# Wider query and key pieces in two attention stages, and the first stage's row normalisation on POOL

## What is computed

```
x = x + 0.5 * ffn0(layernorm(x))     stage 0, "f0": 512 -> 1536 -> 512, silu(gate) * up, weights rounded through fp8
x = x + attn0(layernorm(x))          stage 1, "a0": 16 query heads, 4 key/value heads of 32, a rotary factor, biases
x = x + 0.5 * ffn0(layernorm(x))     stage 2, "f0", same weights
x = x + 0.5 * ffn1(layernorm(x))     stage 3, "f1": 512 -> 2048 -> 512
x = x + attn1(layernorm(x))          stage 4, "a1": 16 query and 16 key/value heads
x = x + 0.5 * ffn1(layernorm(x))     stage 5, "f1"
layernorm(x) = (x - mean) / sqrt(var + 1e-5);   attention is causal, softmax over keys
```

## Time and profile before

| | |
|---|---|
| median of 3 runs | 2639.78 us (2636.49 to 2643.28) |
| the profiled execution's own time | 2630.22 us |
| its span, first to last instruction | 2628.5 us |
| mean granted TensorE clock | 0.994 |
| busy: PE, DVE, ACT, POOL | 2530.7, 1528.6, 1045.8, 966.4 us |
| stage 0 begins its products | 33.3 us |
| a0: opening from 299.6, last of it about 795 us | |
| a1: opening from about 1570, last of it about 2100 us | |

### The profile page before, as it was taken

How to read it: one execution, slowest core, us unless ns; L and a number is a source line. 1 busy time by engine, 2 the same in 40 slices (tenths; PEclk the granted TensorE clock), 3 DMA queues, 4 the chain that set the end, 5 groups by cost and what they waited for, 6 DMA issues and landing times.

```text
span 2628.5 us, 44135 instructions
## 1 busy us (share of the span) xinstructions
PE 2530.7 (96%) x16928; PEld 2010.6 (76%) x16928; DVE 1528.6 (58%) x3356; ACT 1045.8 (40%) x1901; POOL 966.4 (37%) x1357
## 2 busy tenths in 40 slices
PE   6999989989999999999999999999999899999999
PEld 4788867667668888888888878777777678888887
DVE  7777579979975445433333345798589643333333
ACT  7555346655653223311111133566466431111111
POOL 3333566766644225211111122666366521111110
PEclk9999999999999999999999999999999999999999
DMA  4222031132220110100000002342133100000001
GB/s 148 73 73 73 31 83 46 51 72 61 50 90 1 37 45 14 36 25 25 24 25 25 24 17 58 92 97 73 48 93 78 38 33 25 24 25 25 25 16 64
DMA packets 72002, 128.73 MB, mean 49 GB/s; under 512 B 15728, under 2 KB 24944, under 8 KB 71792
## 3 DMA queue, kind: packets, MB, share of 16 engines
q1 hardware_dynamic: 71792, 125.92, 16.9%
HBM read 62.42 MB, written 13.63 MB: 29 GB/s over the span
## 4 chain that ended last, share of the span: by engine, by line
PE 80%; DVE 8%; ACT 2%; POOL 2%; SPq 2%; DMA 2%; issue 2%; DVEq 0%; ACTq 0%; POOLq 0%
PE psum L1045 65%; PE psum L1163 4%; PE psum L1126 4%; PE psum L1144 4%; DVE psum L1495 2%; PE psum L1174 2%; SPq L1726 1%; PE psum L1054 1%; DVE s1a0rden L1534 1%; SPq L1745 1%; DVE s4a1rden L1534 1%; ACT s1a0e L1329 0%; DVE stats L1361 0%; POOL rstd L1604 0%; PE psum L1133 0%
## 5 line engine op out<-in xcount | busy, mean ns | idle before, releaser
L1495 DVE CUSTOM_DVE_ANT_0 psum<-psum,mask_q 128x512 f32<-128x512 f32 (+5 forms) x768 | 413.3, 575 | 100.0 <-PE psum L1126 97.0
L1045 PE MATMUL psum<-hA_hi,wmem 128*128 128x256 f32 (+1 forms) x1536 | 405.5, 334 | 0.5 <-DVE s1a0negmax L1495 0.3
L1045 PEld LDWEIGHTS psum<-hA_hi,wmem 128*128 128x128 f32 x1536 | 270.3, 191 | 32.0 <-DVE s1a0negmax L1495 1.5
L1045 PE MATMUL psum<-hA_lo,wmem 128*128 128x512 f32 (+1 forms) x864 | 293.8, 340 | 0.0
L1329 ACT ACTIVATE s4a1e<-psum,p_scale 128x384 f32<-128x384 f32 (+5 forms) x384 | 205.1, 579 | 92.2 <-PE psum L1144 88.8
L1448 DVE SCALAR_TENSOR_TENSOR x<-psum,x 128x512 f32<-128x512 f32 x256 | 175.8, 689 | 97.2 <-PE psum L1045 93.8
L1329 ACT ACTIVATE s1a0e<-psum,p_scale 128x384 f32<-128x384 f32 (+5 forms) x384 | 201.9, 577 | 76.3 <-PE psum L1144 74.9
L1419 DVE TENSOR_TENSOR s5f1prod<-psum,s5f1silu 128x512 f32<-128x512 f32 x64 | 44.3, 692 | 302.1 <-PE psum L1045 302.1
L1419 DVE TENSOR_TENSOR s3f1prod<-psum,s3f1silu 128x512 f32<-128x512 f32 x64 | 44.3, 692 | 294.1 <-PE psum L1045 294.1
L1616 POOL TENSOR_TENSOR wmem<-raw,wmem 128x512 fp32r<-128x512 f32 x58 | 74.2, 1289 | 314.8 <-ACT wmem L1231 314.7
L1045 PE MATMUL psum<-s3f1w,s3f1a 128*128 128x512 f32 x768 | 181.5, 390 | 0.9 <-POOL s3f1w L1616 0.9
(11 more groups left out here) (194 smaller groups left out, 5568.3 us busy)
## 6 DMA issues: line engine op xcount, KB each, us to landing
s1a0qst<-s1a0qs SPq DMA_DIRECT2D x96, 128.0 KB, 2.4
s4a1qst<-s4a1qs SPq DMA_DIRECT2D x96, 128.0 KB, 2.4
s4a1kst<-s4a1ks SPq DMA_DIRECT2D x96, 128.0 KB, 2.4
raw<-in_gate SPq DMA_DIRECT2D x44, 256.0 KB, 2.9
raw<-in_up SPq DMA_DIRECT2D x44, 256.0 KB, 2.8
raw<-in_down SPq DMA_DIRECT2D x44, 256.0 KB, 2.8
rounded<-s0f0w SPq DMA_DIRECT2D x24, 256.0 KB, 2.0
s2f0w<-rounded SPq DMA_DIRECT2D x24, 256.0 KB, 4.8
```

The costliest lines, as they stand in the source:

```text
L1045: ins = pe.matmul(out_, w, m, start=n == 0, stop=n == len(terms) - 1)
L1495: dve.tensor_tensor_reduce(scores, scores, mask_q[:, first:first + pw], -1.0, -MASKED, ALU.add, ALU.min, T[s]["negmax"][n % 2][:, column:c ...
```

## The change

Pieces become 512 columns wide: two for each name and group where there were four. Products, `turned`, `piece_out` and `piece_lo` each work on 512 columns, with unchanged arithmetic. In the units a piece starts every 4 units where it was every 2; the norm jobs of groups 2 and 6 start one unit earlier. In the opening the guard now holds back the second of two q pieces. Waits that named piece 1 or 3 name the one that covers the same columns. In stage 0 alone `ln_norm` is done by POOL (one `tensor_scalar` of 128x512, multiply then add) and no longer by ACT. The bank model's durations follow.

```diff
+PIECE = 512
+QK_PIECES = SEQ // PIECE
-NORMS_FROM = 11
+NORMS_FROM = 10
-PIECE_STEP = 2
+PIECE_STEP = 4
...
             return [timed((0, ("piece", s, g, n, i)),
...
-                    for i in range(4) for n in names_of_group(s, g)]
+                    for i in range(QK_PIECES) for n in names_of_group(s, g)]
...
-            if norms.busy(last_norm[s, 1]) and any(("piece", s, 0, "q", 2) in job[0]
+            if norms.busy(last_norm[s, 1]) and any(("piece", s, 0, "q", QK_PIECES // 2) in job[0]
...
-            done["norm", s, where[0]] = work("act", 0.81, ("stats", s, where[0]))
+            done["norm", s, where[0]] = work("pool" if s == 0 else "act", 1.3 if s == 0 else 0.81,
+                                             ("stats", s, where[0]))
...
-            done[step] = work("pe", 1.4, *banks)
+            done[step] = work("pe", 1.4 * PIECE / 256, *banks)
...
+        def normed_by_pool(s):
+            return s == 0
...
             def piece(s, g, n, i):
-                cols = slice(i * CH // 2, (i + 1) * CH // 2)
+                cols = slice(i * PIECE, (i + 1) * PIECE)
...
-                products(ps[:, 0, 0:CH // 2], [(wv[wp][:, k, :], hA[hp][:, k, cols])
+                products(ps[:, 0, 0:PIECE], [(wv[wp][:, k, :], hA[hp][:, k, cols])
...
             def ln_norm(s, t):                      # ACT
+                if normed_by_pool(s):
+                    return
...
             def piece_out(s, g, n, i):              # ACT; turned and piece_lo on DVE likewise
-                cols = slice(i * CH // 2, (i + 1) * CH // 2)
+                cols = slice(i * PIECE, (i + 1) * PIECE)
...
+            def ln_norm(s, t):                      # POOL
+                if not normed_by_pool(s):
+                    return
+                k = tmp_place["ln_norm", s, t]
+                if k >= TMPS:
+                    on.wait_ge(*tmp_read(k - TMPS))
+                on.wait_ge(*x_done(s - 1, t))
+                on.wait_ge(sem["ln_rs"], at("ln_rs", "ln_stats", s, t))
+                on.wait_ge(sem["ln_sh"], at("ln_sh", "ln_stats", s, t))
+                pool.tensor_scalar(tmp[k % TMPS][:], x[:, t, :], rstd[:, t:t + 1],
+                                   shift[:, t:t + 1], ALU.mult,
+                                   ALU.add).then_inc(sem["ln_nm"], 1)
...
             def stack(s, g, n, j):                  # SP
-                on.wait_ge(sem["qk_lo"], at("qk_lo", "piece_lo", s, g, n, 3))
+                on.wait_ge(sem["qk_lo"], at("qk_lo", "piece_lo", s, g, n, QK_PIECES - 1))
```

More of the change, by code:

```diff
@@ L1083, in piece @@
                 first, b = 0 if n == "q" else 2, g // HPG
-                cols = slice(i * CH // 2, (i + 1) * CH // 2)
+                cols = slice(i * PIECE, (i + 1) * PIECE)
                 ps = bank_of(("piece", s, g, n, i))
                 on.wait_ge(*w_ready(s, n, g))
-                on.wait_ge(sem["ln_lo"], at("ln_lo", "ln_lo", s, (2 * b + i // 2) * CT + CT - 1))
+                on.wait_ge(sem["ln_lo"], at("ln_lo", "ln_lo", s, (2 * b + i * PIECE // CH) * CT + CT - 1))
                 wv = [wmem[:, g % 2, first + p, :].rearrange("p (k m) -> p k m", k=KT)
                       for p in range(2)]
-                products(ps[:, 0, 0:CH // 2], [(wv[wp][:, k, :], hA[hp][:, k, cols])
+                products(ps[:, 0, 0:PIECE], [(wv[wp][:, k, :], hA[hp][:, k, cols])
                                                for k in range(KT) for wp, hp in THREE],
@@ L1284, in piece_out @@
                     on.wait_ge(sem["rope"], at("rope", "turned", s, g, n, i))
-                    act.activation(dst, buf[:, 0:CH // 2], ACT.Copy).then_inc(sem["qk_hi"], 1)
+                    act.activation(dst, buf[:, 0:PIECE], ACT.Copy).then_inc(sem["qk_hi"], 1)
                 else:
-                    src = psum[:, banks["piece", s, g, n, i][0], 0:CH // 2]
+                    src = psum[:, banks["piece", s, g, n, i][0], 0:PIECE]
                     on.wait_ge(sem["proj"], at("proj", "piece", s, g, n, i))
@@ L1461, in turned @@
                 on.wait_ge(sem["proj"], at("proj", "piece", s, g, n, i))
-                dve.scalar_tensor_tensor(tmp[k % TMPS][:, 0:CH // 2], src, col,
+                dve.scalar_tensor_tensor(tmp[k % TMPS][:, 0:PIECE], src, col,
                                          t["rope"][n][:, cols], ALU.add,
@@ L1472, in piece_lo @@
                 on.wait_ge(sem["qk_hi"], at("qk_hi", "piece_out", s, g, n, i))
-                src = psum[:, banks["piece", s, g, n, i][0], 0:CH // 2]
+                src = psum[:, banks["piece", s, g, n, i][0], 0:PIECE]
                 if STAGES[s] == "a0":
                     buf = tmp_of(("turned", s, g, n, i))
-                    dve.tensor_tensor(lo, buf[:, 0:CH // 2], hi.bitcast(F32),
+                    dve.tensor_tensor(lo, buf[:, 0:PIECE], hi.bitcast(F32),
                                       ALU.subtract).then_inc(sem["qk_lo"], 1)
@@ L1663, in gpsimd_program @@
             steps = {"begin": begin, "open": open_, "ln_stats": ln_stats, "w_split": w_split,
-                     "down": down, "e_add": e_add, "k_ones": k_ones, "bias_x": bias_x,
+                     "down": down, "ln_norm": ln_norm, "e_add": e_add, "k_ones": k_ones, "bias_x": bias_x,
                      "e_mask": e_mask}
```

9 lines of the change are left out of this document (5 added, 4 removed).

## The result

| kernel | median of its runs | ratio to before |
|---|---|---|
| before | 2639.31 us (2634.01 to 2644.20, 17 runs) | 1 |
| changed | 2646.42 us (2637.62 to 2651.73, 17 runs) | 1.0027, 95% interval 1.0019 to 1.0035 |

A forecast was written before the change was run, and what follows sets the result against it. PE was taken as the limit, 96% busy, with DVE limiting groups 2 and 6 of attention stages. Product -5.2, emptying 0, a0 opening -2.1, a1 stacks -1.5, stage 0 -1.0 gave -9.8: 2639.8 to 2630.0 us, range 2617 to 2648.

The forecast's parts named there:

- Part 2: Emptying the pieces on DVE and ACT: less DVE work against longer waits for products, 0 together, bounds -8 and +17 us.
- rival C: DVE-limited attention groups: long products starve DVE, 20 pieces at 1.33 us, 2656.6 us, or 2648 at two thirds; chance 0.13.
- rival D: Stage 0: POOL's norm and DVE exclude each other, 0.82 us in 16 tiles, 2640 us, no change; chance 0.07.
- Part 4: Opening of a1 and units: earlier stacks save 1.5 us of PE's 2.9 us waits; norm jobs one unit earlier cost nothing.
- Part 1: Piece products on PE: 512-column matmuls save 0.10 us a pair, 5.2 us in all; the skill's formula gave 1.6 us.
- rival B: Bodies: the shorter product is hidden by PE's other waits, only opening and half of Part 1 remain, 2635 us; chance 0.17.
- Part 3: Opening of a0: k's stack goes 3 us earlier, at 325.5, and PE's 2.12 us wait disappears, 2.1 us gained.
- the case against: Opening of a0: second chunk's tiles, held by the guard, come late and two turns lack a piece; price 1.4 us.
- Part 5: Stage 0's norm on POOL: 1.3 us each, start unchanged, 1.0 us gained after 33.3 us, bounds 0 and 4.5.
- the term of +0.5 us: Start of stage 0: tile 7's norm takes 0.5 us more on POOL, offset by -0.5 us from lighter ACT.
- rival A: More comes: DVE's relief counts (-8 us) and half of the clock (-1 us), 2621 us; chance 0.16.

The follow-up runs named there:

- e9: Changed kernel with row_min as a reduction with one SBUF input instead of a minimum with two: 2633.84 us, 0.9997 of before.
- e6: Kernel before with only the norm jobs beside the heads starting at unit 10, not 11: 2639.68 us, 1.0011 of before.
- e5: Changed kernel with the norm jobs beside the heads starting at unit 11 again, not 10: 2640.52 us, 1.0010 of before.
- e11: Changed kernel with the one-input reduction for row_min and the norm jobs from unit 11: 2632.08 us, 0.9981 of before.
- e14: e11 with the norms of stage 0 on ACT again instead of POOL: 2635.21 us, 0.9989 of before.
- e1: Kernel before with only stage 0's norm moved to POOL, its bank model duration included: 2637.64 us, 1.0005 of before.
- e2: Changed kernel with turned, piece_out and piece_lo one unit later in the units, opening unchanged: 2649.56 us, 1.0047 of before.
- e7: Changed kernel with pieces emptied one unit later from group 1 on and norms from unit 11: 2646.58 us, 1.0036 of before.
- e4: Changed kernel with a piece's twelve matmuls issued as six and, two units later, six, into the same bank: 2651.98 us, 1.0059 of before.

## Why the prediction was wrong, step by step

**The step that failed is Part 2, "I take 0 for both together".** It weighed two things against each other, less DVE work and a longer wait for the product, and for both it counted lengths. Both came: the work fell by 18.3 us, and DVE's waits at `turned` in the body of a0 rose from 12.3 to 22.3 us. What decided was an instruction it did not name. The pieces moved the rows and with them `row_min` by some tenths of a microsecond against POOL's additions. In the bodies that took 9.5 us (a0) and 4.3 us (a1) more of DVE, and 10.4 us more of the chain that ended last. Taking the hold away is worth 1.0027 - 0.9997 = 0.0030, 7.9 us, in the changed kernel and 0.0004, no measurable change, in the kernel before.

That the measured time lies within 2 us of rival C's 2648 is luck: C's sign, over 1.5 us of DVE idle before `turned`, came true (2.1 us in groups 2 and 6 of a0), and in e9, where it is as long, the kernel is no slower than before.

The prediction had the mechanism at hand: rival D told it of stage 0, from the earlier trace rows, and asked of the new instruction alone whom it would meet. It should have asked it of every pair of DVE steps with two SBUF inputs and POOL steps that the change moves against each other. The group of `row_min` (404 and 580 ns in the mean where a single one takes 160) showed that this pair met already. The Trainium skill, SBUF — State Buffer, section Who interferes with whom, states the rule for just these kinds of instruction; the trace agrees, with 1.86 against 0.16 us, and e9 with 0.16 us for one SBUF input beside the same addition.

**"The norm jobs one unit earlier: no cost seen" (Part 4) was the second.** Timed, it costs 0.0011 (e6) to 0.0017 (1.0027 - 1.0010, e5; e9 against e11 gives 0.0016), 3 to 4.5 us, each of the three barely clear of noise or not quite. I had looked for the statistics' releaser, not for what the head had already on ACT and PE.

**Part 1, the product: right in price, but in a0's undisturbed groups nothing of it arrived.** Twelve matmuls of 512 columns took 2.75 us, as the chain after shows:

```profile
1632.28 2.75 PE psum L1052 x12
...
1637.11 1.85 DVE s4a1negmax L1513
```

The undisturbed head of e9, 11.48 for 11.59 us, is the saving of 0.10 to 0.11 a pair, as the rows had it and not the 0.03 that Part 1 gave beside it. The second line is what ate it: `row_min` is now a link of the chain itself. And without the lock the head behind eats it: an undisturbed group of four heads in a0 takes 48.51 us in e9 and 48.47 before. In these groups that is rival B, the saving hidden behind other waits, and the 5.2 us of the sum did not come from them.

**Part 3, the opening of a0: right in mechanism, too large.** k's stack goes at 326.94 (expected 325.5, before 328.46), the first row has no idle time before it any more, 2.12 us before:

```profile
324.89 1.87 SPq L1748 DMA_DIRECT2D s1a0qst<-s1a0qs  x3
326.94 1.77 SPq L1748 DMA_DIRECT2D s1a0kst<-s1a0ks  x3
...
330.62 0.47 PE L1133 MATMUL psum<-s1a0kst,s1a0qst 96*128 96x512 f32 x1
```

But the start had come 1.5 us earlier by itself. Counted from PE's first product k's stack goes as before (295.1 us in both), and this row comes after 298.8 us for 298.9. A new wait of 1.50 us at 314.95, where q's second piece stands for the transposed tiles, took most of the gain: the second chunk's tiles came late, which I had named as the case against. Another 1.7 us went to the clock. In the 11 other profiles with wide openings the stretch took 296.8 to 299.2 us, 297.5 in the median. So 1.4 us is the fairer figure, and it has to cover Part 5's 1.0 us and the opening's share of Part 1 as well.

**Part 4, a1's stacks: right in mechanism.** The 2.9 us of waits for `s4a1kst` are gone from the list of a1's waits. The 1.5 us of the sum can't be checked: whatever they gave lies under the loss of a1's body (+5.5 us).

**Part 5, the norm on POOL: price too high, gain too low.** The form takes 0.80 us in the mean, not 1.3:

```profile
L1628 POOL TENSOR_SCALAR tmp<-x,rstd,shift 128x512 f32<-128x512 f32 x16 | 12.8, 799 | 2.8 <-POOL shift L1616 2.8
```

That is the price on ACT (0.81), so the term of +0.5 us vanishes and the start comes 1.5 to 2 us earlier (e14 against e11 shows whose doing it is). The windows of the rest of stage 0 are 265.8 us for 266.3, half a microsecond of the 1.0 I had counted. Rival D's meeting took place, but once before PE's start and not eight times (POOL's norm, then the rounding step with two SBUF inputs; start, us):

```profile
30.25 0.77 POOL L1628 TENSOR_SCALAR tmp<-x,rstd,shift 128x512 f32<-128x512 f32 x1 [0.20 <-POOL shift L1616]
...
30.52 1.04 DVE L1400 SCALAR_TENSOR_TENSOR s0f0cbase<-s0f0cbig,s0f0clow 128x512 bf16<-128x512 bf16 x1
```

The same step took 0.67 to 0.69 us elsewhere in these 33 us. The meeting is there in e1 and e9 too (1.03 us) and not in the kernel before; it cost DVE 0.36 us, and the sign I had named, a step over 1 us in the first 33 us, could not tell one meeting from eight.

**The clock** was left out except in rival A, and as a gain. About two thirds of the difference between the two profiled spans is clock: 2644.7 x 0.010 - 2628.5 x 0.006 = 26.4 - 15.8 = 10.6 of 16.2 us. New stalls of PE were in places followed by a stretch at the lower clock, as at 354 and 474 us, and no part of the sum had a price for that.

**What is left of the forecast.** 2630.0 of 2639.8 is a ratio of 0.9963. The lock (0.0030) and the early norms (0.0016) account for the way from 1.0027 to e11's 0.9981. The last 0.0018, some 5 us, is what the terms of the sum were too large by; the profiles point to Part 1 and Part 3.

What stays open: why e2 and e7, whose undisturbed heads are as good as before, lose 0.0020 to 0.0026 on their counterparts (after and e5) with DVE starved of rows instead, and e4 more (the banks are a candidate that no run tests, though PE's waits for `piece_lo`, which frees a piece's bank, are 1.4 us in e2 and none in e4); what keeps the third head 0.16 us long in e9; and what sets the clock, which took back the gain of e1.

## What to carry to other kernels

Where a step of one engine can be held by another's, list every pair of instructions that can meet, not only the new one, and look for the pairs whose mean duration is above the shortest: a change that shifts the work by a few tenths of a microsecond moves them onto or off the path. A tiny instruction on the critical path, here four elements a partition, is worth giving a form that was not held. And cut a loop's body at a marker that comes once a turn: the turn that grew points to the cause, which sums over a stage hide. Keep the clock's share apart as well, over all runs and not in one profile each: the profile of the kernel before had 6 us less of it than its runs had in the mean.

## What the runs showed of the hardware

- A DVE step of 128x4 with two SBUF inputs took 0.16 us when it started with POOL's addition, and 1.86 us when it started 0.26 us behind it, until the addition ended. All 38 such steps of the changed kernel that took over 0.3 us ended within 0.06 us of the end of an addition on POOL. A reduction 128x8 to 128x4 with one SBUF input took 0.16 us in 64 of 64 places, 51 of them beside such additions.
- POOL's tensor_scalar on 128x512 with two operands of one value a partition took 0.77 to 0.80 us, against 1.41 us for an addition with two full inputs.
- Behind waits of PE of 1.0 and 1.6 us close to each other the granted clock of the next 8 us was 0.57 in the mean; in e5, with one wait of 1.46 us in that head, it stayed at 1.00.
